# A two-layer graph attention with a routed FFN: 20 of 49 node tiles get their FFN densely inside the second edge phase

## What is computed

```python
x = x + gnn(_layernorm(x), edge_index, ...)      # both attention layers
logits = xf @ gate_w + gate_b                    # xf = _layernorm(x)
probs = softmax(logits); top2_vals, top2_idx = top_k(probs, 2)
cw = zeros((N, 8)).at[arange(N)[:, None], top2_idx].add(top2_vals)
for e in range(8):                               # D = 256, H = 512
    out += cw[:, e, None] * (gelu(xf @ W1[e] + b1[e]) @ W2[e] + b2[e])
x = x + out
```

## Time and profile before

| | us |
|---|---|
| median of three runs (lowest to highest) | 4742.56 (4742.23 to 4744.06) |
| span of the profiled execution, first to last instruction | 4740.9 |
| first gather of edge phase 1 to the last of phase 2 | 132.3 to 4169.4 |
| up matmuls of the expert phase, first to last start | 4238.5 to 4672.3 |
| combining adds, first to last start | 4685.9 to 4737.1 |

### The profile page before, as it was taken

How to read it: one execution, slowest core, us unless ns; L and a number is a source line. 1 busy time by engine, 2 the same in 40 slices (tenths; PEclk the granted TensorE clock), 3 DMA queues, 4 the chain that set the end, 5 groups by cost and what they waited for, 6 DMA issues and landing times. The chain is left out here.

```text
span 4740.9 us, 66856 instructions
## 1 busy us (share of the span) xinstructions
PE 3346.1 (71%) x12675; PEld 2411.6 (51%) x12676; DVE 2922.4 (62%) x7641; ACT 1673.7 (35%) x3999; POOL 3342.4 (71%) x3623
## 2 busy tenths in 40 slices
PE   6577676666676666674667777677777667759994
PEld 5455454444554444453455555455555455537673
DVE  7766666666666666666666666666666666654445
ACT  4333333333333333332333333333333333322223
POOL 5777777777777777776777777777777777747323
PEclk8777777777777777777777676767777777769997
DMA  5555555555555555544555555555555555554325
GB/s 162 141 139 140 139 140 138 140 139 140 140 140 140 138 139 140 139 127 123 144 146 146 145 144 145 146 146 145 145 144 144 145 145 145 147 171 143 94 82 192
DMA packets 312156, 669.34 MB, mean 141 GB/s; under 512 B 74233, under 2 KB 137653, under 8 KB 311812
## 3 DMA queue, kind: packets, MB, share of 16 engines
q0 software_dynamic: 170464, 468.31, 37.1%
q1 hardware_dynamic: 141039, 199.89, 14.6%
q10 hardware_dynamic: 596, 0.53, 0.0%
HBM read 601.32 MB, written 75.12 MB: 143 GB/s over the span
## 5 line engine op out<-in xcount | busy, mean ns | idle before, releaser
L1155 POOL DMA_INDIRECT rows<-table,idx x3192 | 3017.8, 945 | 981.2 <-issue 925.8
L1311 PE MATMUL bank<-rows,hit 128*128 128x260 f32 (+1 forms) x6448 | 2494.9, 544 | 1191.1 <-DVE acc L1426 1180.0
L1311 PEld LDWEIGHTS bank<-rows,hit 128*128 128x128 f32 x6448 | 1645.9, 272 | 1740.2 <-DVE acc L1426 1370.0
L1411 DVE TENSOR_TENSOR rows<-rows,bank 128x1024 f32<-128x1024 f32 x808 | 947.7, 1214 | 36.9 <-ACT rows L1191 36.9
L1188 ACT ACTIVATE arg<-arg 128x32 f32<-128x32 f32 (+1 forms) x404 | 88.4, 219 | 2383.3 <-DVE arg L1404 2383.3
L1426 DVE TENSOR_TENSOR acc<-acc,bank 128x260 f32 (+1 forms) x2016 | 842.4, 418 | 30.6 <-PE bank L1311 3.0
L1397 DVE TENSOR_TENSOR arg<-rows,bank 128x32 f32<-128x32 f32 (+1 forms) x404 | 71.6, 177 | 1155.1 <-DMA rows<-table,idx 1154.8
L1377 DVE TENSOR_TENSOR hit<-bank,dst_at 128x256 f32<-128x256 f32 x1616 | 672.0, 417 | 0.0
L1182 ACT ACTIVATE hit_t<-gap,ones 128x1024 bf16<-128x1024 bf16 x404 | 463.8, 1148 | 27.3
L1175 ACT ACTIVATE gap<-loc,minus_node 128x1024 bf16<-128x1024 bf16 x404 | 462.7, 1145 | 10.9 <-DMA loc<-loc_row 10.6
L1296 PEld LDWEIGHTS bank<-du,hit_t 128*128 128x128 bf16 x3232 | 249.2, 109 | 248.7 <-issue 180.1
(11 more groups left out here) (289 smaller groups left out, 2249.2 us busy)
## 6 DMA issues: line engine op xcount, KB each, us to landing
loc<-loc_row SPq DMA_DIRECT2D x404, 256.0 KB, 3.6
rows<-table,idx POOLq DMA_INDIRECT x3192
sent<-zeros SPq DMA_DIRECT2D x202, 68.3 KB
xe<-sent SPq DMA_DIRECT2D x106, 128.5 KB
got<-back SPq DMA_DIRECT2D x48, 256.0 KB, 5.2
fw<-in_L_ffn_W SPq DMA_DIRECT2D x16, 512.0 KB
table<-acc POOLq DMA_DIRECT2D x49, 130.0 KB
table<-acc SPq DMA_DIRECT2D x49, 128.5 KB, 2.3
```

Of the source, the lines that this page charges most:

```text
L1155: pool.indirect_dma_start(rows[:, way, n, 0:R], None, table, bass.IndirectOffsetOnAxis(idx[:, way, n:n + 1], 0)).then_inc(rows_in[way], 16)
L1311: last = nc.tensor.matmul(sum_bank[(way + m) % 4][:, 0:R], hit[:, way, n, :], rows[:, way, n, 0:R], start=(n == UNITS[m][0]), stop=(n == U ...
L1411: nc.vector.tensor_tensor(r, r, weight[:, some, :].unsqueeze(3).to_broadcast([P, PIECE, H, D // H]), ALU.mult).then_inc(scaled, 1)
```

## The change

**What it does.**
- The first DENSE = 20 tiles of `tile_order` leave the routed FFN. They get all 8 experts, densely, during edge phase 2, in GROUPS = 5 groups of GROUP = 4 tiles. One expert of one group takes one turn (4 steps, `part` 0 to 3), so 5 x 8 turns = 160 steps, from step DENSE_AT = 34 on. A turn holds four up pieces (128 hidden features of 512 tokens: 2 matmuls of 512 columns), each followed by a Gelu on ACT out of PSUM with the bias in it, and four down pieces (one tile each: a bias matmul of one row and 4 matmuls of 256 columns), each followed by one DVE operation that adds it, times the gate's share, into `total`. All pieces use the one PSUM bank that the edge weights had, so each piece waits for the one before to be read.
- Each step of edge phase 2 has two pieces on PE: `dense(at, 1)` behind `spread_du`, in front of unit 1, and `dense(next_at, 0)` in front of unit 4.
- SP loads an expert's weights once a turn (512 KB up, 512 KB down, one buffer each), and per group `total` from and to memory. `mid_x` and the logits are now kept in `tile_order`.
- In edge phase 2 `make_hit` and `scale_rows` are gone. Eight `tensor_scalar` operations build the one-hot with the weight in it (`is_equal`, then `mult`), after `weigh`; the column next to the rows is set to one by ACT.
- ACT needs the Gelu table as well; a small exp (`exp_table_first`) is put in front of `weigh` in the two steps with Gelus.
- `LAG` is 4 in both edge phases, so the last two tiles are finished one after the other behind the last step.
- The router, the slots and the combining hold the other TAIL = 29 tiles; SLOT_TILES is 66. ACT first copies the 29 tiles' rows into an array of their own (`move_y`). The partial tile is put last in the order.

**The diff, cut to its core.**

```diff
-SLOT_TILES = (2 * N + EXPERTS * (P - 1)) // P
+LAST_KEY = float(1 << 24)
+DENSE = 20
+GROUP = 4
+GROUPS = DENSE // GROUP
+TAIL = NT - DENSE
+TOKENS = N - DENSE * P
+SLOT_TILES = (2 * TOKENS + EXPERTS * (P - 1)) // P
...
-    LAG = 3
+    LAG = 4
...
+    DENSE_AT = SETS * (GROUP + LAG) + 2
+    PER_GROUP = EXPERTS * SETS
...
+                def load_up(e, n):
+                    if not number(n) or n >= 1:
+                        sp.wait_ge(up_made, n * CHUNKS)
+                    sp.dma_start(up_w[:, :, :], fw1[e].rearrange("(c p) n -> p c n", p=P)).then_inc(up_w_in, 16)
+
+                def load_down(e, n):
+                    if not number(n) or n >= 1:
+                        sp.wait_ge(down_made, n * GROUP)
+                    sp.dma_start(down_w[:, :, :], fw2[e].rearrange("(c p) n -> p c n", p=P)).then_inc(down_w_in, 16)
+                    sp.dma_start(down_b[:, :], fb2[e].unsqueeze(0)).then_inc(down_w_in, 16)
...
-                    nc.scalar.activation(weight, a, ACT.Exp, scale=-1.0)
-                    nc.scalar.activation(rows[:, way, :, D:D + H], a, ACT.Exp, scale=-1.0).then_inc(weight_ready, 1)
+                    if first_layer:
+                        nc.scalar.activation(weight, a, ACT.Exp, scale=-1.0)
+                        nc.scalar.activation(rows[:, way, :, D:D + H], a, ACT.Exp, scale=-1.0).then_inc(weight_ready, 1)
+                    else:
+                        nc.scalar.activation(edge_weight[:, way % 2, :], a[:, :, 0], ACT.Exp, scale=-1.0).then_inc(weight_ready, 1)
+                        nc.scalar.copy(rows[:, way, :, D], kp.ones[:, 0:ST]).then_inc(ones_set, 1)
...
+                def bend(at, c):
+
+                    g, e, part, n = at
+                    if e == 0 and c == 0:
+                        act.wait_ge(up_b_in, 16)
+                    act.wait_ge(up_made, n * CHUNKS + c + 1)
+                    nc.scalar.activation(inner[:, c, :], dense_bank[:, 0:GROUP * P], ACT.Gelu,
+                                         bias=up_b[:, e * CHUNKS + c:e * CHUNKS + c + 1]).then_inc(inner_ready, 1)
...
+                    if bends:
+                        bend(at, 2 * at[2])
+                        nc.scalar.activation(exp_first[:, :], kp.ones[:, 0:1], ACT.Exp)
                     if not number(s) or s + 1 < STEPS:
                         weigh(s + 1, (way + 1) % SETS)
+                    if bends:
+                        bend(at, 2 * at[2] + 1)
...
+                def dense(at, half):
+
+                    g, e, part, n = at
+                    if part < 2:
+                        c = 2 * part + half
+                        if c == 0:
+                            pe.wait_ge(up_w_in, n * 16 + 16)
+                            pe.wait_ge(down_taken, n * GROUP + 1)
+                            if e == 0:
+                                pe.wait_ge(turned_kept, g * GROUP + GROUP)
+                        else:
+                            pe.wait_ge(inner_ready, n * CHUNKS + c)
+                        for kc in range(2):
+                            last = nc.tensor.matmul(
+                                dense_bank[:, 0:GROUP * P], up_w[:, kc, c * P:(c + 1) * P],
+                                turned_y[:, kc, bass.ds(g * GROUP, GROUP), :].rearrange("p a n -> p (a n)"),
+                                start=(kc == 0), stop=(kc == 1))
+                        last.then_inc(up_made, 1)
+                    else:
+                        i = 2 * (part - 2) + half
+                        if i >= GROUP:
+                            return
+                        if i == 0:
+                            pe.wait_ge(down_w_in, n * 32 + 32)
+                            pe.wait_ge(inner_ready, n * CHUNKS + CHUNKS)
+                        else:
+                            pe.wait_ge(down_taken, n * GROUP + i + 1)
+                        nc.tensor.matmul(dense_bank[:, 0:D], kp.ones[0:1, :], down_b[:, :], start=True, stop=False)
+                        for c in range(CHUNKS):
+                            last = nc.tensor.matmul(dense_bank[:, 0:D], inner[:, c, i * P:(i + 1) * P], down_w[:, c, :],
+                                                    start=False, stop=(c == CHUNKS - 1))
+                        last.then_inc(down_made, 1)
...
+                    if not first_layer:
+                        for n in range(some.start, some.stop):
+                            last = nc.vector.tensor_scalar(hit[:, way, n, :], col, dst_at[:, way, n:n + 1],
+                                                           edge_weight[:, way % 2, n:n + 1], ALU.is_equal, ALU.mult)
+                        last.then_inc(scaled, 1)
+                        return
```

More of the change, by code:

```diff
@@ new lines, in dense @@
+                def dense(s, at):
+                    if number(s) and s == 12:
+                        with nc.allow_non_contiguous_dma(reason="biases along the partitions"):
+                            sp.dma_start(up_b[:, :], fb1.rearrange("e (c p) -> p (e c)", p=P)).then_inc(up_b_in, 16)
+                    if number(s) and s == 24:
+                        load_up(0, 0)
+                    if number(s) and s == 26:
+                        load_down(0, 0)
+                    if number(s) and s == DENSE_AT + 1:
+                        sp.wait_ge(mid_out, 16 * GROUP)
+                        for h in range(2):
+                            load_total(0, h)
+                    if at is None:
+                        return
+                    g, e, part, n = at
+                    if part == 0 and not (number(n) and n == 0):
+                        load_up(e, n)
+                    if part == 2 and not (number(n) and n == 0):
+                        load_down(e, n)
@@ L1250, in ride, with step @@
                         keep_y(turn - LAG)
-                def step(s, way, turn):
+                def step(s, way, turn, at=None):
+                    bends = at is not None and at[2] < 2
                     if not number(s) or s + 3 < STEPS:
@@ L1696, in load @@
                         sp.wait_ge(home_ready, k - 1)
-                    if not number(k) or turn * 4 + after < NT:
+                    if not number(k) or turn * 4 + after < TAIL:
                         sp.wait_ge(second_sent[after % 4], (turn + after // 4 + 1) * 16)
```

395 lines of the change are left out of this document (304 added, 91 removed).

## The result

| | us |
|---|---|
| before, median (lowest to highest) | 4742.59 (4742.23 to 4744.06) |
| after, median (lowest to highest) | 4575.69 (4572.83 to 4580.04) |
| ratio after/before, 95% interval | 0.965, 0.9636 to 0.9664 |
| span of the profiled execution, before and after | 4740.9 and 4573.3 |

The change makes the kernel 167 us faster. The prediction said 4567 us, the range 4553 to 4690.

What follows compares the result with a forecast made beforehand. POOL's gather issue rate was taken to bound edge phase 2, PE the expert phase. From 4740.9 us, less 188, plus 8 for tails and 4 for edges: span 4564.9, median 4567 us, range 4553 to 4690.

Steps and rivals of the forecast that it cites:

- POOL's issue rate is the bound: Edge phase 2: gathers issued 1.25 us apart, 40.0 us a turn, set the pace before and after the change.
- What is taken away: Expert phase: 40 fewer slot tiles 164 us, 20 fewer combining tiles 21, shorter router 3; sum 188 us.
- The clock: PE in edge phase 2: mean granted clock rises from 0.71 to above 0.9, so no loss in the dense stretch.
- Rival (b): Dense stretch: PE's clock stays at 0.71, a turn takes 53.5 us, 540 us more, 5107 us; chance 0.11.
- Rival (a), PE as the bound: Dense stretch: PE, at 38.0 of 40.0 us a turn, becomes the bound; 4647 or 4656 us; chance 0.24.
- ACT: Edge phase 2: table loads, Gelus and copies raise ACT's busy time from 15.8 to 25.5 of 40 us a turn.
- Rival (c), the gathers: Layer 2: the eight `tensor_scalar` a step slow POOL's gathers, 107 us (4674) or 444 us (5011); chance 0.05.
- DVE is no bound: Edge phase 2: DVE's busy time goes from 6.3 to about 4.9 us a step.
- The router, -3: Expert phase: the router's operations shrink from 392 to 232 elements, saving 3 us (0 to 5).
- The combining, priced by DVE's adds alone: End of the expert phase: 29 tiles for 49 at 1.07 us a tile on DVE, 21 us less.
- Layer 1's tail, 3.5 for 6.3: Behind layer 1's last step: one more tile finished with LAG = 4, 3.5 us; 8 us with layer 2's 4.8.
- The edges of the dense stretch, +4 for -1.1: Edge phase 2: gate choice per group and biases arriving in 4-byte pieces, allowed 4 us (0 to 15).

Runs made afterwards that it cites:

- e1: Changed kernel without the dense FFN of the 20 tiles and its weight loads in edge phase 2; 4574.74 us, ratio 0.9643.
- e8: Changed kernel with DENSE = 16 for 20: four groups, 74 slot tiles for 66; 4625.66 us, ratio 0.9733.
- e3: Changed kernel with all four up pieces of a turn computed twice, 7.6 us more on PE; 4732.32 us, ratio 0.9972.
- e10: Changed kernel with both pieces of a step one behind the other behind the spreads, in front of unit 1; 5052.61 us, ratio 1.0653.
- e7: Changed kernel without the small exp (`exp_table_first`) that brings ACT's table in early; 4585.48 us, ratio 0.9647.
- e5: Changed kernel with a plain one-hot in edge phase 2 and rows scaled by two tensor_tensor operations, weights in SBUF; 4704.51 us, ratio 0.9905.
- e11: As e5, but the rows are scaled by eight `tensor_scalar` operations with the weight as scalar; 4590.99 us, ratio 0.9658.
- e12: Changed kernel with odd combining stores on SP and expert-phase biases loaded as single rows and spread on the chip; 4575.69 us, ratio 0.9626.
- e6: Changed kernel with the eight one-hot `tensor_scalar` operations reading column numbers from SBUF instead of PSUM; 4587.62 us, ratio 0.9655.

## Why the prediction was right

**Right, and shown.**
- *POOL's issue rate is the bound, and stays it.* 1441 gathers in 1800 us. e1 has the same time without the dense work.
- *What is taken away.* Slot tiles -164.5 us for 164, adds -21.5 for 21. e8 gives 39 us for a group of four, 37 by the same prices.
- *The clock.* 0.98 in the dense stretch; "above 0.9 and PE busy above 93%" were its signs, 94% came. Rival (b) did not happen. e1 has 0.76 in the same stretch, so it is the filled gaps that bring the clock up.
- *Rival (a), PE as the bound.* It starts only with 3.7 us more PE work a turn (e3). PE needs at most 36.3 us a turn where the sum had 38.0, so there was more room than the 0.24 that I gave this rival supposed. The spreads show a part of this: in the full stretch of e3 they take 105.9 us in 34.2 turns, 3.1 us a turn with hardly any idle time in front, where the sum had 4.0, 1.2 of it issue.
- *ACT.* 25.4 us a turn (954.24 / 1500 x 40) for 25.5. The drain of 1.38 us that the Trainium skill adds to each switch (ScalarE: Activation LUTs, "What ACT_TABLE_LOAD costs") does not show: in e10's timeline the small exp starts 1.30 us behind the start of its load (3009.65 to 3010.95), and the sum by the rows was met. The moved `exp` was worth nothing (e7).
- *Rival (c), the gathers.* In after layer 2's take 0.2 us more than layer 1's, so it did not happen. But the prediction's sentence that a gather takes 0.94 to 1.01 us whatever the other engines do holds only beside the operations of before: in e5 it takes up to 2.0 us. (Beside edge phase 2 stand 1596 gathers, not the 1616 of the rival's price.)
- *DMA.* The share is 0.59 in the dense stretch where some 0.65 was forecast, and DVE's wait for landed rows got shorter, as said.
- *DVE is no bound.* True, with e11, although its busy time is 6.1 us a step for the 4.9 predicted: the eight new operations take 2.6 us a step (532.8 us in 202 steps) where I took 2.2, and I had subtracted whole groups whose operations partly overlap their neighbours' on the timeline; what each of the two makes of the 1.2 us is not separated.
- *Pieces well placed.* e10: the same matmuls in one place cost 476 us.

**Terms that were off,** between the predicted span of 4564.9 and the measured 4573.3, 8.4 us:
- *The router, -3.* It got 4.3 us shorter, but with the 4.7 us that the sends wait longer nothing is left: a term on a path that did not set the end. e12 shows that transfers did, for a part of it.
- *The combining, priced by DVE's adds alone.* The store's address is new work for POOL, which now stands 0.64 us or more between two stores (0.24 to 0.53 before, where it kept pace), and POOL became the slower engine: +6.8 us. This was in the diff, and I had not costed it. Of a moved or changed step every engine's part needs its own rate.
- *Layer 1's tail, 3.5 for 6.3.* The projection belongs to the chain. Layer 2's was 4.0 for 4.8.
- *The edges of the dense stretch, +4 for -1.1.* Layer 2's gathers take no longer than before; the gate's choice and the scattered biases are hidden. The last gather came 6.4 us later than before, for the 4 of the forecast's signs, and it was the start and layer 1's tail that moved it.
- The plan's new operations cost 1.1 us at the start.

The prediction's lines and the measured ones differ by 16.2 us one way (1.1 at the start, 0.1 in layer 1, 2.8 in its tail, 4.7 in front of the first up matmul, 0.7 in front of the first add, 6.8 at the end) and by 8.2 the other (5.1 at the edges, 0.8 in layer 2's tail, 1.3 in the router, 0.5 each in the slot tiles and the adds). The 8.0 that are left are the 8.4 to within rounding. So the mechanism and the two large terms were right, and that the total came within 9 us is in part luck: an allowance of 4 us that nothing needed stood against costs that the sum had at nothing.

## What to carry to other kernels

Where an engine that issues transfers sets the pace, others' idle time can hold work at no cost, but only if each piece is finished before the queues of the other engines come to it: price a place by what stands behind the waiting instruction on every engine, not by the wait itself. When a stage shrinks, its second engine is next: the combining went from DVE's rate to POOL's at once, and the expert phase's start did not follow its router, since transfers held a part of it. A scaling with a broadcast second tensor should have that tensor in PSUM, or be done with a scalar operand, where POOL issues gathers beside it.

## What the runs showed of the hardware

- A DVE `tensor_tensor` of 1.22 us with both inputs in SBUF lets a gather's issue on POOL grow from 0.95 to up to 2.0 us; the same with one input in PSUM does not (longest 1012 ns), nor does `tensor_scalar` from SBUF to SBUF with its scalars (e6 and e11, longest 1067 and 1081 ns). These two lengthen a gather by 4 and 3 ns in the mean, 6.4 and 5.3 us over the layer's 1596, measured against the other layer in the same trace.
- The gathers of layer 1, which no edit touches, take 1508 to 1509 us together in eight of the fourteen traces (945 to 946 ns each) and 1512 to 1514 in the other six (947 to 948 ns). Over both layers that is up to 10 us, as much as some of the differences between the kernels above, so small ones are better read within one trace than from the total.
- PE's busy share overstates its need: at 94% busy, 3.7 us more work in a turn of 40 us, 9%, still fitted (e3).
